# Attention scores for two light items at once, and the products with V of two items in front of them

## Chip, cores and metric

One core of one Trainium2 chip. The time is the device time of one execution in microseconds. The kernel before takes 2064.11 us, the median of three runs (2062.43 to 2066.58).

## What is computed

The input is x, 8 sequences of 1024 tokens with 256 features, in f32. Three residual blocks follow each other:

```
x = x + 0.5 * moe(layernorm(x))        # 8 experts of 128 hidden units, the best 2 per token
x = x + attention(layernorm(x))
x = x + 0.5 * moe(layernorm(x))
```

Attention has 8 heads of 64 and two branches whose outputs are added:

```
light: q, k, v = split(layernorm(x) @ wqkv); windows of 64 queries see 3 windows of 64 keys
       out = softmax(q k^T / 8) v @ wo_l                                    # all 1024 tokens
heavy: the 256 tokens with the highest scores x . rt_q are the queries,
       the 256 with the highest scores x . rt_kv are keys and values (rms-normed x)
       out = softmax(q k^T / 8) v @ wo_h, added back at the query tokens
```

## The kernel before

The program is written out by hand for the five engines (TensorE, ScalarE, VectorE, GpSimd, SyncE), with semaphores between them. The first block routes tokens to experts through memory (the first 371 us of the span), attention takes the time up to some 1610 us, and the last block computes all experts densely. The change touches attention alone.

Attention runs sequence after sequence, 0 to 7. A sequence has 40 items. An item is one tile of 128 queries and one pair of heads: 32 light items (8 tiles by 4 pairs) and then 8 heavy ones (2 tiles by 4 pairs). Each item sees 256 keys; for light ones a mask cuts the windows.

All engines walk through the same list of slots, `slots()`, one item per slot. In slot u:

- TensorE computes the scores of item u (`scores`, two heads, each with half of the array's rows: 64x128 tiles), the transposes of item u-3's probabilities (`turn`, full array) and the products with V of item u-4 (`values`, two heads, each with half of the array's columns: 128x64 tiles).
- VectorE adds the mask, copies the scores to `prob` and finds their maxima (`maxima(u)`), copies the turned probabilities of odd items from PSUM (`turned(u-3)`), and inverts the sums of item u-1.
- ScalarE computes the exponentials (`exps(u)`) and copies the turned probabilities of even items (`turned(u-3)`).
- GpSimd multiplies item u-1's probabilities with the inverse sums (`prob_norm`).

Between these stand jobs, listed per slot by `attn_jobs(u)`: projections to q, k and v of the same sequence and of the next (`qkv`), turned rows of the next sequence (`zt`), its routing scores (`srow`), the gather and the projections of the heavy branch (`ga`, `hp`), and the output product of a finished tile (`op`). TensorE does the first job of a slot after the scores, the second after the transposes, the others after the products with V. The jobs take PSUM banks 6 and 7 in turn, and `claim(job)` waits until the bank's job before the last has been copied out, mostly by ScalarE. A slot's jobs are the same in sequences 0 to 6 but for small shifts. Slots 2, 16, 18, 24, 30, 36 and 39 have none, slots 5, 9, 17, 27 and 33 only an output product or a heavy projection, slot 19 a gather, slots 20, 21, 23, 25 and 29 three or more. VectorE has, besides, the additions of the first block's results and the statistics for the next sequence (slots 1 to 19) and the ranking of tokens by pairwise comparison (`rank_piece`, slots 22 to 39 and 0 to 7). GpSimd has 16 gathers by indirect DMA in slots 35 to 39 and 0 to 10 and 16 scatters in slots 36 to 39, 0 to 3 and 9 to 16. Sequence 7 has no next one, so most of the jobs and of this other work are missing there.

The scores of item j, head h, go to `bank[g % NS]` with g = 2 * j + h and NS = 3, in columns 0 to 255. `scores(j)` waits for the reader of what the bank held before: score g - 3, that is the maxima (light) or the exponentials (heavy) of an item at most two before. `probT` has one buffer for even items and one for odd ones; `turn(j)` waits until item j-2's turned probabilities have been copied out of its bank, and the copy of item j waits for `values(j-2)`.

Of the kernel before, what the change touches and what calls it, by code (L numbers as in the profile page):

```python
# [31 lines left out]
LIGHT, SLOTS = 32, 40  # L32
# [6 lines left out]
def build(nc, x_in, gamma_h, wq_h, wkv_h, wo_h, ln_g, ln_b, wqkv, wo_l, rt_q, rt_kv,  # L39
# [4 lines left out]
    T = N // P  # L44
# [18 lines left out]
    MAXB, MAXI = max(BLOCKS), max(r1 - r0 for r0, r1 in BATCH) * N // BLK  # L63
    NH = 3
    NP = 4
    NS = 3
    assert FF == P and KEYS == NSEL and HC == 4 and TG == 4 and C == 2

    ctx = ExitStack()
    with ctx:  # L70
# [39 lines left out]
        mask = sb("mask", [P, 3, KEYS], BF16)  # L110
# [275 lines left out]
        def is_item(u):  # L386
            return 0 <= u < SLOTS * ROWS
# [91 lines left out]
        def tile_at(j):  # L479
            if not 0 <= j < 40 * ROWS:  # L480
                return None, None
            b, i = divmod(j, 40)
            return 10 * b + i // HP, i % HP

        def heavy_tile(n):
            return n % 10 >= T
# [241 lines left out]
        def pe_program():  # L728
# [232 lines left out]
            def scores(j):  # L961
                n, hp = tile_at(j)
                b, t = divmod(n, 10)
                if t < T:
                    if hp == 0 and t in (0, 3, 4):
                        pe.wait_ge(s_qkv, 25 * b + {0: qkv_with(0, 0), 3: qkv_with(1, 1), 4: qkv_with(0, 1)}[t])
                    if j == 0:
                        pe.wait_ge(s_halo, 2)
                        pe.wait_ge(s_by, STEPS)
                elif t == T and hp == 0:  # L970
                    pe.wait_ge(*left(("hp", b, 3)))
                for h in range(2):
                    g = 2 * j + h

                    if g >= NS:
                        if heavy_tile(tile_at((g - NS) // 2)[0]):
                            pe.wait_ge(s_soft, g - NS + 1)
                        else:
                            pe.wait_ge(s_nm, g - NS + 1)
                    hs = slice(h * DH, (h + 1) * DH)  # L980
                    if t < T:
                        ins = pe.matmul(bank[g % NS][:, 0:KEYS], qT[hs, hp, t * P:(t + 1) * P], kT[hs, hp, t * P:t * P + KEYS], start=True, stop=True)  # L982
                    else:
                        ins = pe.matmul(bank[g % NS][:, 0:KEYS], hq[hs, hp, (t - T) * P:(t - T + 1) * P], hk[hs, hp, :], start=True, stop=True)  # L984
                    ins.then_inc(s_sim)

            def turn(j):
# [73 lines left out]
                    job(*what)  # L1061
            for u in slots():
                todo = attn_jobs(u)
                if is_item(u):
                    scores(u)
                for what in todo[0:1]:
                    job(*what)
                if is_item(u - 3):
                    turn(u - 3)
                for what in todo[1:2]:  # L1070
                    job(*what)
                if is_item(u - 4):
                    values(u - 4)
                for what in todo[2:]:
                    job(*what)
                if u in EARLY.values():
                    ffn_hidden((u - SLOTS * ROWS) // 2)
            for k in range(GROUPS):
# [3 lines left out]
        def act_program():  # L1082
# [225 lines left out]
            def exps(j):  # L1308
                n, hp = tile_at(j)
                if j >= 4:  # L1310
                    act.wait_ge(s_rden, j - 3)
                light = n % 10 < T
                if not light:
                    act.wait_ge(s_tp, j - NP + 1)
                for h in range(2):
                    g = 2 * j + h
                    act.wait_ge(s_nm, g + 1)
                    src = prob[j % NP][:, h, :] if light else bank[g % NS][:, 0:KEYS]
                    act.activation(prob[j % NP][:, h, :], src, ACT.Exp, bias=nmax[:, j % 4, h:h + 1], scale=-1.0 if light else 1.0,  # L1319
                                   accum_out=den[:, j % 4, h:h + 1]).then_inc(s_soft)  # L1320

            def turned(j):

                if j % 2:
                    return
                act.wait_ge(s_tp, j + 1)
                if j >= 2:
                    act.wait_ge(s_pv, j - 1)
                act.activation(probT[j % 2][:, :, :], view(3 + j % 2, "p (a n) -> p a n", a=4), ACT.Copy).then_inc(s_pt[0])
# [49 lines left out]
            for u in slots():  # L1379
                todo = attn_jobs(u)  # L1380
                if is_item(u):
                    exps(u)
                for what in todo[0:1]:
                    evac(*what)
                if is_item(u - 3):
                    turned(u - 3)
                for what in todo[1:]:
                    evac(*what)
                if is_item(u - 4) and (u - 4) % HP == HP - 1:
                    values_left(tile_at(u - 4)[0])  # L1390
# [16 lines left out]
        def dve_program():  # L1407
# [360 lines left out]
            def maxima(j):  # L1768
                n, hp = tile_at(j)
                t = n % 10  # L1770
                if j >= 4:
                    dve.wait_ge(s_soft, 2 * (j - 3))
                if t < T and j >= NP:
                    dve.wait_ge(s_tp, j - NP + 1)
                which = 0 if t == 0 else 2 if t == T - 1 else 1
                for h in range(2):
                    g = 2 * j + h
                    dve.wait_ge(s_sim, g + 1)
                    if t < T:
                        ins = dve.tensor_tensor_reduce(prob[j % NP][:, h, :], bank[g % NS][:, 0:KEYS], mask[:, which, :], -1.0, 3e38, ALU.add, ALU.min, nmax[:, j % 4, h:h + 1])  # L1780
                    else:
                        ins = dve.tensor_reduce(nmax[:, j % 4, h:h + 1], bank[g % NS][:, 0:KEYS], AX_X, ALU.max, negate=True)
                    ins.then_inc(s_nm)

            def turned(j):

                if j % 2 == 0:
                    return
                dve.wait_ge(s_tp, j + 1)
                if j >= 2:  # L1790
                    dve.wait_ge(s_pv, j - 1)
                dve.tensor_copy(probT[j % 2][:, :, :], view(3 + j % 2, "p (a n) -> p a n", a=4)).then_inc(s_pt[1])  # L1792
# [350 lines left out]
```

## Time and profile before

| | |
|---|---|
| Median of three runs | 2064.11 us |
| The profiled execution | 2061.01 us, its span 2059.2 us |
| TensorE busy | 1875.1 us |
| VectorE busy | 1388.5 us |
| ScalarE busy | 1203.6 us |
| GpSimd busy | 1172.0 us |
| Mean granted clock of TensorE | 0.977 of 2.4 GHz |

The profile is one execution. A timeline row merges instructions of one line that follow each other without a gap; its first number is the start from the span's beginning. PEld is TensorE's weight load. A start of item 0's scores in a sequence marks the sequence's beginning: 371.00, 530.84, 690.43, 847.25, 1004.95, 1164.58, 1322.22 and 1479.02 us.

### The profile page before, as it was taken

How to read it: one execution, taken by the hardware profiler on the slowest of the kernel's cores; microseconds unless marked ns; L12 is line 12 of the kernel's file. 1: busy time of each engine (PE TensorE's matmuls, PEld its weight loads, DVE VectorE, ACT ScalarE, POOL GpSimd, SP SyncE). 2: the span in 40 equal slices, each digit the busy share in tenths (PEclk: the TensorE clock that was granted, in tenths of full speed). 3: DMA queues.
4: the chain of work that ended last, by engine and by line, in shares of the span. 5: the costliest groups of instructions: out<-in, count | busy, mean ns of one | idle time of the engine just before them, and what ended most of it. 6: DMA issues, size and time to landing. Idle time of an engine off the chain costs nothing.

```text
span 2059.2 us, 38092 instructions
## 1 busy us (share of the span) xinstructions
PE 1875.1 (91%) x11764; PEld 1398.7 (68%) x11764; DVE 1388.5 (67%) x4771; ACT 1203.6 (58%) x2974; POOL 1172.0 (57%) x1356
## 2 busy tenths in 40 slices
PE   3488899889989989989989989989999999999998
PEld 1166678656656666666666666666666788888887
DVE  5355457756855865875874875775754488888887
ACT  5487567565565565565566566566555555555554
POOL 3999852662772782782682683583453444444444
PEclk8599999999999999999999999999999999999999
DMA  6688887200310310310310220220121111111110
GB/s 200 248 267 289 275 267 251 67 27 1 100 40 1 98 42 1 95 45 1 93 47 1 81 55 5 77 57 8 37 63 82 38 42 42 42 42 42 36 38 21
DMA packets 103841, 168.15 MB, mean 82 GB/s; under 512 B 13249, under 2 KB 64857, under 8 KB 102745
## 3 DMA queue, kind: packets, MB, share of 16 engines
q1 hardware_dynamic: 80600, 112.91, 16.8%
q0 software_dynamic: 20736, 52.52, 8.1%
q8 instruction: 97, 1.59, 0.3%
q14 instruction: 104, 0.84, 0.1%
q10 hardware_dynamic: 2304, 0.28, 0.1%
HBM read 80.33 MB, written 85.34 MB: 80 GB/s over the span
## 4 chain that ended last, share of the span: by engine, by line
PE 51%; DVE 16%; POOL 10%; issue 10%; ACT 9%; DMA 4%; ACTq 0%; SPq 0%; DVEq 0%; POOLq 0%
PE bank L730 7%; PE bank L732 6%; PE bank L731 6%; PE bank L1022 4%; PE bank L1011 4%; PE bank L982 4%; PE bank L993 4%; PE bank L953 3%; PE bank L890 2%; ACT prob L1319 2%; PE bank L872 2%; POOL prob L2005 2%; DVE st L1412 2%; POOL spots_d L1952 2%; PE bank L984 2%
## 5 line engine op out<-in xcount | busy, mean ns | idle before, releaser
L2005 POOL TENSOR_TENSOR prob<-prob,rden 128x512 f32<-128x512 f32 x320 | 337.6, 1056 | 453.8 <-DVE rden L1798 450.2
L1319 ACT ACTIVATE prob<-prob,nmax 128x256 f32<-128x256 f32 x512 | 256.0, 502 | 391.3 <-DVE nmax L1780 383.5
L1780 DVE CUSTOM_DVE_ANT_0 prob<-bank,mask 128x256 f32<-128x256 f32 x512 | 195.3, 417 | 103.3 <-PE bank L982 97.3
L1666 DVE SCALAR_TENSOR_TENSOR xb<-bank,gate,xb 128x256 f32<-128x256 f32 x512 | 211.8, 476 | 55.6 <-PE bank L732 55.1
L1932 POOL TENSOR_TENSOR hl<-hf,hh 128x512 fp32r<-128x512 f32 x128 | 164.7, 1291 | 113.8 <-ACT hh L1122 109.1
L982 PE MATMUL bank<-kT,qT 64*128 64x256 f32 x1024 | 211.2, 431 | 14.3 <-DVE nmax L1780 13.6
L993 PE MATMUL bank<-ident,prob 128*128 128x128 f32 x1280 | 198.8, 278 | 16.1 <-POOL prob L2005 16.1
L993 PEld LDWEIGHTS bank<-ident,prob 128*128 128x128 f32 x1280 | 154.3, 142 | 73.7 <-POOL prob L2005 26.5
L1121 ACT ACTIVATE hf<-bank,b1s 128x512 f32<-128x512 f32 x128 | 88.2, 689 | 171.2 <-PE bank L732 167.7
L1792 DVE COPY probT<-bank 128x512 f32<-128x512 f32 x160 | 110.0, 688 | 113.7 <-PE bank L993 112.8
L1011 PE MATMUL bank<-probT,V 128*64 128x128 f32 x2048 | 169.7, 287 | 9.0 <-ACT oT_s L1335 7.1
L1992 POOL DMA_INDIRECT hs_d<-yr,place x128 | 130.0, 1016 | 43.4 <-issue 31.0
L1952 POOL DMA_INDIRECT spots_d<-xb,spot x128 | 126.3, 987 | 49.4 <-DVE spot L1513 28.4
L1011 PEld LDWEIGHTS bank<-probT,V 128*64 128x64 f32 x2048 | 108.2, 137 | 64.5 <-issue 61.3
L730 PE MATMUL bank<-w,hh 128*128 128x256 f32 x512 | 146.6, 286 | 3.7 <-POOL hl L1932 2.6
L982 PEld LDWEIGHTS bank<-kT,qT 64*128 64x128 f32 x1024 | 94.0, 186 | 77.7 <-issue 47.1
L732 PE MATMUL bank<-w,hh 128*128 128x256 f32 x512 | 144.7, 283 | 0.0
L731 PE MATMUL bank<-w,hl 128*128 128x256 f32 x512 | 144.5, 282 | 0.0
L1812 DVE TENSOR_TENSOR x<-bank,x 128x256 f32<-128x256 f32 x64 | 27.0, 422 | 147.0 <-PE bank L1022 147.0
L1578 DVE TENSOR_TENSOR yout<-bank,b_all 128x512 f32<-128x512 f32 x85 | 58.1, 690 | 100.5 <-PE bank L890 62.0
L1022 PE MATMUL bank<-wol,oT_s 128*128 128x256 f32 x512 | 125.8, 388 | 0.0
L730 PE MATMUL bank<-xt_hi,wqkv_hi 128*128 128x512 f32 x256 | 114.1, 446 | 0.0
(256 smaller groups left out, 5044.7 us busy)
## 6 DMA issues: line engine op xcount, KB each, us to landing
xin<-spots_d SPq DMA_DIRECT2D x85, 256.0 KB
made_d<-yout SPq DMA_DIRECT2D x85, 256.0 KB
x<-in_L_attn_x SPq DMA_DIRECT2D x8, 1024.0 KB
x_d<-x SPq DMA_DIRECT2D x8, 1024.0 KB, 4.5
xb<-x_d SPq DMA_DIRECT2D x16, 512.0 KB, 3.9
out<-xb SPq DMA_DIRECT2D x16, 512.0 KB, 3.0
xb<-in_L_attn_x SPq DMA_DIRECT2D x7, 1024.0 KB, 6.7
spots_d<-zeros SPq DMA_DIRECT2D x24, 256.0 KB
```

Of the source, the lines that this page charges most:

```text
L730: pe.matmul(o, w[0], x[0], start=start, stop=False)
L731: pe.matmul(o, w[1], x[0], start=False, stop=False)
L732: return pe.matmul(o, w[0], x[1], start=False, stop=stop)
L982: ins = pe.matmul(bank[g % NS][:, 0:KEYS], qT[hs, hp, t * P:(t + 1) * P], kT[hs, hp, t * P:t * P + KEYS], start=True, stop=True)
L993: ins = pe.transpose(bank[3 + j % 2][:, (2 * h + kk) * P:(2 * h + kk + 1) * P], prob[j % NP][:, h, kk * P:(kk + 1) * P], ident[:, :])
L1011: ins = pe.matmul(bank[5][h * DH:(h + 1) * DH, hp * P:(hp + 1) * P], V[:, t + kk, hs] if t < T else hv[:, kk, hs], probT[j % 2][:, 2 * h + ...
L1022: ins = pe.matmul(bank[tb][:, 0:D], oT_s[:, ch, :], w[:, ch, :], start=(ch == 0), stop=(ch == HC - 1))
L1319: act.activation(prob[j % NP][:, h, :], src, ACT.Exp, bias=nmax[:, j % 4, h:h + 1], scale=-1.0 if light else 1.0, accum_out=den[:, j % 4, ...
L1666: dve.scalar_tensor_tensor(out=x, in0=bank[ob][:, (t % 2) * D:(t % 2 + 1) * D], scalar=gate[:, k % 2, t, e:e + 1], in1=x, op0=ALU.mult, op ...
L1780: ins = dve.tensor_tensor_reduce(prob[j % NP][:, h, :], bank[g % NS][:, 0:KEYS], mask[:, which, :], -1.0, 3e38, ALU.add, ALU.min, nmax[:, ...
L1952: pool.indirect_dma_start(spots_d[batch_of_row(r)], bass.IndirectOffsetOnAxis(spot[:, r, c, t:t + 1], 0), xb[r % 4][:, t, :], None).then_i ...
L2005: pool.tensor_tensor(prob[j % NP][:, :, :], prob[j % NP][:, :, :], rden[:, j % 4, :].unsqueeze(2).broadcast_to([P, 2, KEYS]), ALU.mult).th ...
```

## The change

Light items 2i and 2i+1 form a set, and each heavy item is a set alone, 24 sets per sequence. A set uses two of the three banks, one per head; the even item of a light set writes columns 0 to 255, the odd one 256 to 511. TensorE computes the scores of both items in the even slot and none in the odd one. It waits, once per set and head, for the readers of what the banks held. VectorE's maxima wait until the set's last item has been computed for that head. The products with V of the two items u-5 and u-4 stand at the end of odd slots, after all jobs; in even slots there are none. All further jobs of a slot follow directly after the transposes. ScalarE copies the turned probabilities of even items one slot later, in slot u of item u-4, after the exponentials of slot u and ahead of all of its jobs. VectorE's copies of the odd items stay.

```diff
+        SETS = LIGHT // 2 + SLOTS - LIGHT
+        def set_of(j):
+            b, i = divmod(j, SLOTS)
+            return SETS * b + (i // 2 if i < LIGHT else i - LIGHT // 2)
+        def set_end(n):
+            b, i = divmod(n, SETS)
+            return SLOTS * b + (2 * i + 1 if i < LIGHT // 2 else i + LIGHT // 2)
+        def score_place(j, h):
+            n, side = ((0, 1), (2, 0), (1, 2))[set_of(j) % 3][h], 0 if heavy_tile(tile_at(j)[0]) else j % 2
+            return bank[n][:, side * KEYS:(side + 1) * KEYS]
...
                 for h in range(2):
-                    g = 2 * j + h
-                    if g >= NS:
-                        if heavy_tile(tile_at((g - NS) // 2)[0]):
-                            pe.wait_ge(s_soft, g - NS + 1)
-                        else:
-                            pe.wait_ge(s_nm, g - NS + 1)
+                    old = set_end(set_of(j) - 2 + h)
+                    if old >= 0 and (j == 0 or set_of(j - 1) != set_of(j)):
+                        pe.wait_ge(s_soft if heavy_tile(tile_at(old)[0]) else s_nm, 2 * old + (1 - h) + 1)
...
                 todo = attn_jobs(u)
-                if is_item(u):
-                    scores(u)
+                if is_item(u) and (u == 0 or set_of(u - 1) != set_of(u)):
+                    for j in range(u, set_end(set_of(u)) + 1):
+                        scores(j)
                 for what in todo[0:1]:
                     job(*what)
                 if is_item(u - 3):
                     turn(u - 3)
-                for what in todo[1:2]:
+                for what in todo[1:]:
                     job(*what)
-                if is_item(u - 4):
+                if u % 2 and is_item(u - 4):
+                    values(u - 5)
                     values(u - 4)
-                for what in todo[2:]:
-                    job(*what)
...
                 if is_item(u):
                     exps(u)
+                if is_item(u - 4):
+                    turned(u - 4)
                 for what in todo[0:1]:
                     evac(*what)
-                if is_item(u - 3):
-                    turned(u - 3)
...
                 for h in range(2):
                     g = 2 * j + h
-                    dve.wait_ge(s_sim, g + 1)
+                    dve.wait_ge(s_sim, 2 * set_end(set_of(j)) + h + 1)
```

The other lines put `score_place(j, h)` where `bank[g % NS][:, 0:KEYS]` stood.

## Rows read from the trace of the kernel before

**Rows 1.** The page's first part: busy time, share of the span, instructions of TensorE.

```profile
PE 1875.1 (91%) x11764; PEld 1398.7 (68%) x11764; DVE 1388.5 (67%) x4771; ACT 1203.6 (58%) x2974; POOL 1172.0 (57%) x1356
```

**Rows 2.** Stretches: length, busy time per engine (instructions), clock, DMA. Sequences 1, 3, 7.

```profile
530.84:690.43 159.59, 149.20 (x952) 103.25 (x951) 108.96 (x419) 94.61 (x271) 94.35 (x105) 0.99 0.16 46
847.25:1004.95 157.70, 147.23 (x952) 101.91 (x951) 108.59 (x419) 94.70 (x271) 94.45 (x105) 1.00 0.16 46
1479.02:1606.91 127.89, 124.26 (x850) 86.68 (x849) 69.34 (x282) 71.97 (x218) 60.68 (x61) 0.97 0.19 66
...
847.25:895.17 47.92, 46.37 (x294) 31.96 (x292) 42.43 (x163) 27.83 (x83) 39.91 (x46) 1.00 0.30 85
```

**Rows 3.** Timeline of TensorE, sequence 3, slots 14 and 15: start, length, what.

```profile
904.75 0.60 PE L993 MATMUL bank<-ident,prob 128*128 128x128 f32 x4
905.28 0.66 PE L1011 MATMUL bank<-probT,V 128*64 128x128 f32 x8
905.87 0.70 PE L982 MATMUL bank<-kT,qT 64*128 64x256 f32 x4
906.50 0.50 PE L730 MATMUL bank<-wqkv_hi,xt_hi 128*128 128x512 f32 x1
906.84 0.39 PE L731 MATMUL bank<-wqkv_hi,xt_lo 128*128 128x512 f32 x1
...
908.00 0.60 PE L993 MATMUL bank<-ident,prob 128*128 128x128 f32 x4
908.43 0.60 PE L900 MATMUL bank<-ident,z_row 128*128 128x128 f32 x4
```

**Rows 4.** Timeline, sequence 3, slots 22 and 23: TensorE, then VectorE, then ScalarE.

```profile
935.80 0.70 PE L982 MATMUL bank<-kT,qT 64*128 64x256 f32 x4
...
944.29 1.97 PE L953 MATMUL bank<-hin,wqh 128*128 128x256 f32 x8 [1.49 <-ACT kT L1276]
946.18 0.70 PE L982 MATMUL bank<-kT,qT 64*128 64x256 f32 x4
...
936.67 0.42 DVE L1780 CUSTOM_DVE_ANT_0 prob<-bank,mask 128x256 f32<-128x256 f32 x1 [0.27 <-PE bank L982]
...
938.57 0.69 DVE L1792 COPY probT<-bank 128x512 f32<-128x512 f32 x1 [1.12 <-PE bank L993]
...
942.06 0.41 DVE L1780 CUSTOM_DVE_ANT_0 prob<-bank,mask 128x256 f32<-128x256 f32 x1
...
942.57 0.51 ACT L1319 ACTIVATE prob<-prob,nmax 128x256 f32<-128x256 f32 x1 [3.80 <-DVE nmax L1780]
...
943.57 0.57 ACT L1276 ACTIVATE kT<-bank 128x512 f32<-128x512 f32 x1
944.04 0.58 ACT L1329 ACTIVATE probT<-bank 128x512 f32<-128x512 f32 x1
```

**Rows 5.** Timeline of TensorE, sequence 3, slots 12 and 13: transposes of items 9, 10.

```profile
894.00 0.66 PE L993 MATMUL bank<-ident,prob 128*128 128x128 f32 x4 [0.77 <-POOL prob L2005]
...
897.84 0.66 PE L993 MATMUL bank<-ident,prob 128*128 128x128 f32 x4 [1.38 <-POOL prob L2005]
```

**Rows 6.** Stretches around two long waits of TensorE; the third number from the end is the clock.

```profile
424.80:431.00 6.20, 3.90 (x15) 2.93 (x16) 0.86 (x6) 4.68 (x13) 3.12 (x4) 0.72 0.08 29
...
1543.00:1554.00 11.00, 7.63 (x31) 5.36 (x31) 4.89 (x24) 6.55 (x20) 3.71 (x6) 0.69 1.03 419
```

**Rows 7.** Timeline of TensorE behind the first of these waits.

```profile
427.13 0.76 PE L730 MATMUL bank<-wqkv_hi,xt_hi 128*128 128x512 f32 x1 [2.30 <-ACT xf_t L1265]
427.69 0.63 PE L731 MATMUL bank<-wqkv_hi,xt_lo 128*128 128x512 f32 x1
428.12 0.63 PE L732 MATMUL bank<-wqkv_lo,xt_hi 128*128 128x512 f32 x1
```

**Rows 8.** Timeline, sequence 3: maxima of item 18, then TensorE's scores of item 20.

```profile
918.28 0.42 DVE L1780 CUSTOM_DVE_ANT_0 prob<-bank,mask 128x256 f32<-128x256 f32 x1
...
921.01 0.83 PE L982 MATMUL bank<-kT,qT 64*128 64x256 f32 x4
```

More of the change, by code:

```diff
@@ L65, in build @@
     NP = 4
-    NS = 3
     assert FF == P and KEYS == NSEL and HC == 4 and TG == 4 and C == 2
@@ L972, in scores @@
                 for h in range(2):
-                    g = 2 * j + h
-                    if g >= NS:
-                        if heavy_tile(tile_at((g - NS) // 2)[0]):
-                            pe.wait_ge(s_soft, g - NS + 1)
-                        else:
-                            pe.wait_ge(s_nm, g - NS + 1)
+                    old = set_end(set_of(j) - 2 + h)
+                    if old >= 0 and (j == 0 or set_of(j - 1) != set_of(j)):
+                        pe.wait_ge(s_soft if heavy_tile(tile_at(old)[0]) else s_nm, 2 * old + (1 - h) + 1)
                     hs = slice(h * DH, (h + 1) * DH)
                     if t < T:
-                        ins = pe.matmul(bank[g % NS][:, 0:KEYS], qT[hs, hp, t * P:(t + 1) * P], kT[hs, hp, t * P:t * P + KEYS], start=True, stop=True)
+                        ins = pe.matmul(score_place(j, h), qT[hs, hp, t * P:(t + 1) * P], kT[hs, hp, t * P:t * P + KEYS], start=True, stop=True)
                     else:
-                        ins = pe.matmul(bank[g % NS][:, 0:KEYS], hq[hs, hp, (t - T) * P:(t - T + 1) * P], hk[hs, hp, :], start=True, stop=True)
+                        ins = pe.matmul(score_place(j, h), hq[hs, hp, (t - T) * P:(t - T + 1) * P], hk[hs, hp, :], start=True, stop=True)
                     ins.then_inc(s_sim)
@@ L1317, in exps @@
                     act.wait_ge(s_nm, g + 1)
-                    src = prob[j % NP][:, h, :] if light else bank[g % NS][:, 0:KEYS]
+                    src = prob[j % NP][:, h, :] if light else score_place(j, h)
                     act.activation(prob[j % NP][:, h, :], src, ACT.Exp, bias=nmax[:, j % 4, h:h + 1], scale=-1.0 if light else 1.0,
@@ L1777, in maxima @@
                     g = 2 * j + h
-                    dve.wait_ge(s_sim, g + 1)
+                    dve.wait_ge(s_sim, 2 * set_end(set_of(j)) + h + 1)
                     if t < T:
-                        ins = dve.tensor_tensor_reduce(prob[j % NP][:, h, :], bank[g % NS][:, 0:KEYS], mask[:, which, :], -1.0, 3e38, ALU.add, ALU.min, nmax[:, j % 4, h:h + 1])
+                        ins = dve.tensor_tensor_reduce(prob[j % NP][:, h, :], score_place(j, h), mask[:, which, :], -1.0, 3e38, ALU.add, ALU.min, nmax[:, j % 4, h:h + 1])
                     else:
-                        ins = dve.tensor_reduce(nmax[:, j % 4, h:h + 1], bank[g % NS][:, 0:KEYS], AX_X, ALU.max, negate=True)
+                        ins = dve.tensor_reduce(nmax[:, j % 4, h:h + 1], score_place(j, h), AX_X, ALU.max, negate=True)
                     ins.then_inc(s_nm)
```

## Prediction, written before the changed kernel ran

> **What bounds the kernel now.** I read the page first: TensorE is busy 91% of the span [rows 1], so the first question is which part of a slot on TensorE is work and which is not. The stretch table comes next [rows 2]: the whole of sequence 3 takes 157.70 us, of which TensorE is busy 147.23, VectorE 108.59, GpSimd 94.45. Its first twelve slots (47.92 us) look different: VectorE 42.43, GpSimd 39.91 and between GpSimd's DMA issues small gaps that nothing can fill. So slots 0 to 11 are held by three engines at once, slots 22 to 39 by TensorE. Sequence 7, which prepares no next sequence, needs 127.89 us with TensorE busy for 124.26. Last, the timeline of TensorE slot by slot [rows 3], and for single slots that of the other engines [rows 4, 5, 8].
>
> I number by the slot u of its sequence. S is the scores of an item, T its four transposes, V its product with V; "even" and "odd" are the slots of a pair.
>
> **What a change of the array's shape costs.** S uses 64x128 tiles, V 128x64, all else the full array. In [rows 3] T to V is 0.53 us, but T to another full-array group (908.00 to 908.43) 0.43: 0.10 lost on leaving. V takes 0.59 for eight instructions that run in pairs, four steps of 0.108, the step of T's transposes (0.43 for four): 0.15 lost (0.05 entering, 0.10 leaving). S takes 0.63 for two pairs of passes over 256 columns; eight such passes take 1.89 [rows 4], two 0.43: 0.20 lost. The projection's first pass takes 0.34 (906.50 to 906.84), the other five (908.00 - 906.84)/5 = 0.23: 0.10 lost. One round full array, V, S, full array costs 0.10 + 0.15 + 0.20 + 0.10 = 0.55 us, in each slot.
>
> The Trainium skill, TensorEngine Tiling (Array Packing), "Key Properties", says that a change of tiling mode drains the engine. The 0.10 on every leaving side agrees with it. By that rule alone this change is worth all the rounds that it takes out.
>
> **What the change removes.** Per pair of light items one of two rounds goes: 0.55. 128 pairs make 70 us. For heavy pairs only V moves; the round V to S of the even slot becomes T to S: some 0.15, 32 pairs, 5 us. A pair with a projection in each slot would fall from 6.49 to 5.94 us of TensorE time: S S 1.06, projection 1.50, T 0.43, projection 1.39, T 0.53, V V 1.02. This is the gross gain. The rest is what eats it.
>
> **What it adds.** (a) An even slot's maxima start when the second item's scores of that head are there: 0.87 us after S began now (935.80 to 936.67) [rows 4], 0.87 + 0.43 = 1.30 then. (b) T(u-3) of the even slot starts 0.43 later, and behind it VectorE's copy, its extras and the next maxima. (c) ScalarE copies T(u-4) only after exps(u). T(u-2) in the odd slot waits for that copy. Maxima to exps 0.51, two exps 1.00, copy 0.58 (942.06, 942.57, 943.57, 944.04) [rows 4], some 0.15 until TensorE starts: 1.30 + 2.24 = 3.55 us after S S began. With two projections T(u-2) comes at 4.39 and waits for nothing. With one it comes at 2.95 to 3.0, with none in the even slot and a gather in the odd one at 2.0. (d) V no longer stands between jobs. Where a job waits for its bank, V was done in that wait; now TensorE idles, and 1.02 us of V V follow. (e) Idle stretches merge and grow, and with them the clock. DMAs and GpSimd's commands are not moved; they follow the slots.
>
> **Slot by slot, for sequences 0 to 6** (plus is gain):
> Slots 36 to 11: VectorE and GpSimd set the pace [rows 2]; 0 (bounds -0.5 and +1.5; the second if all of S(0)'s gain went through).
> Slots 12, 13: T(9) at 894.00 and T(10) at 897.84 both wait for GpSimd [rows 5], whose chain is untouched. Between them stand now V(8), S(13) and a turn; then only the turn. The output product and V V come after T(10) and end before S(14) is wanted: 0 without the clock.
> Slots 14 to 19: two rounds 1.1, and a wait of V for ScalarE's copy of V's output goes, since V(4n) comes a slot later. But slot 18 has no job and 19 only a gather: maxima(18) at 918.28 [rows 8], T(16) 2.24 behind them, then T and V V, 1.55: S(20) at 922.1 minus what was won before, now 921.01. I take +0.3 up to S(22) without the clock.
> Slots 22, 23: maxima(23) stand behind the copy of T(19) and 3.5 us of rank work (938.57 to 942.06) [rows 4]. They shift by (b), 0.43. The heavy projection waits for the bank that ScalarE empties after exps(23), now at 944.29, 8.49 after S(22); then 8.9. It ends at 10.7, V V at 11.75, where S(24) began after 10.38: -1.4.
> Slots 24, 25: +0.55, less 0.6 by (c): 0. Slots 26 to 29: two rounds 1.1, less 0.4 for S(28), which waits for maxima behind two rank pieces: +0.7. Slots 30, 31: +0.95 with the present 0.5 wait of S(31) gone, less 0.6 by (c): +0.35. Slots 32 to 35: +0.3, given back in 36, 37, where S(37) comes 0.6 us before exps(36).
> Sum without the clock: 0.3 - 1.4 + 0 + 0.7 + 0.35 = 0 per sequence. Sequence 7 has little other work: 0.55 for each of seven pairs with full slots, 0.55 less some 0.28 by (c) for seven shorter ones, against 1.2 lost in the empty heavy slots by the wait of slot 37: +4.5.
>
> **The clock.** In the slot 22/23 pair TensorE has 1.06 + 1.50 + 0.43 + 1.39 + 0.43 + 0.43 = 5.25 us of work before the heavy projection and then stands for 8.9 - 5.3 = 3.6 us. In slots 12/13 it stands from 894.9 to 897.84, 2.9 us. Now the same places are waits of 1.49 and 1.38 [rows 4, 5], and sequence 3 has clock 1.00 [rows 2]. After a wait of 2.30 us [rows 7] the granted clock fell to the 1.2 GHz level: the projection's passes come 0.43 apart (427.69 to 428.12), not 0.23. The stretch around it has a mean of 0.72 [rows 6], so 0.28 x 2 x 6.2 = 3.5 us at half, 1.7 us of work lost; around the wait in sequence 7's slot 20 it is 0.69 over 11 us, 6.8 us at half, 3.4 lost. For slot 23 I take 2.2 (bounds 0 and 3.4): the work behind is dense and on the path. For slot 13 I take 0.8 (0 and 2): part of the loss falls into the wait for the claim of slot 14, the rest delays ScalarE's full queue there. That is 3.0 per sequence, 21 us for seven. Against it, sequences 0, 1 and 4 now lose 2 us each in slot 14 (159.6 against 157.7, clock 0.99 [rows 2]); that wait shrinks, as V V now fill it: +6.
>
> The Trainium skill, TensorE: Matmul & The Clock Gate, Part 1, says that a gap in the work sends the array back to the lower clock. The rows on the 2.30 us wait agree. It speaks against this change; by the tiling rule alone nothing of it would be seen.
>
> **Sum.** Loss 21 - 6 - 4.5 = 10.5 us. The profiled execution took 2061.01 us (span 2059.2), 3.1 under the median 2064.11 of the runs shown: 2071.5 there, 2074.5 as a median, forecast 2074.
>
> **Rivals.**
> 1. The clock holds, or falls in few sequences. For it: waits of 1.4 and 1.5 leave it at 1.00 [rows 2, 4, 5]. Against it: the 2.30 us wait. The shape rounds then stand alone: 0 x 7 + 4.5 + part of the 6: 8 us gained, 2056. Faster.
> 2. Both sides cancel: half of the falls, some sequences as now: within 4 us of 2064.
> 3. The rounds decide, since the waits of (b) to (d) overlap with waits that exist. With everything 1994; with the VectorE-bound and short slots taken out about half, 2030. Against it: VectorE 42.43 of 47.92 us in slots 0 to 11. For it: TensorE is busy 147.23 of 157.70 us. (The tiling rule of the skill alone gives this rival's first number.)
> 4. The fall lasts longer: each of 14 idle stretches costs 3.4, and ScalarE's queue in slots 14 to 21 never catches up: 14 x 3.4 - 10.5 = 37, less what lies in waits: 2090.
> 5. The change doesn't do what it says: V V or S S drain between items too. Nothing in [rows 3] shows that within one shape; it would take the 70 us away and leave the costs, over 2100.
>
> **Chances.** Forecast 0.55 (its own range 2067 to 2084), rival 1 0.19, rival 2 0.12, rival 3 0.06, rival 4 0.06, rival 5 0.02. What a measurement can tell from no change is 0.2%, 4.1 us. Slower: nearly all of the forecast, 4 and 5, 0.61; same: rival 2 and the forecast's lower edge, 0.14; faster: 1 and 3, 0.25. The range leaves out 3 and 5 and the end of 4: 2050 to 2090.
>
> **What would show it.** Right: TensorE idle for over 3 us before the heavy projection of slot 23 in seven sequences, and the granted clock under 1 behind it; S to maxima 1.30 in even slots; S S in 1.06 and V V in 1.02; slots 0 to 11 as long as now; sequence 7 shorter by some 4 us; no wait of V for the output copy in slot 16. Wrong: sequences under 156 us (then a drain was worth more, or the waits less), or a clock of 1.00 throughout, or V V over 1.2.

## Result and profile after

The changed kernel takes 2107.11 us (median of four runs, 2103.06 to 2110.6) against 2064.12: 1.0214 times as long, 95% interval 1.0196 to 1.0232. Forecast were 2074, range 2050 to 2090. The direction was right; the loss of 43 us is over four times the 10.5 forecast. The profiled executions differ by 49.0 us in span (2108.2 and 2059.2).

The page of after: its engine line, which answers to [rows 1], and the row of the transposes (busy us, mean ns | idle time ahead, what ended most of it).

```profile
PE 1848.6 (88%) x11764; PEld 1429.7 (68%) x11764; DVE 1399.4 (66%) x4771; ACT 1203.9 (57%) x2974; POOL 1173.3 (56%) x1356
...
L1008 PE MATMUL bank<-ident,prob 128*128 128x128 f32 x1280 | 204.3, 284 | 88.8 <-ACT probT L1346 60.1
```

TensorE is busy 26.5 us less, though a lower clock (mean 0.960, before 0.977) makes part of its work longer: the rounds that were taken out are gone. The same row on the page of before:

```profile
L993 PE MATMUL bank<-ident,prob 128*128 128x128 f32 x1280 | 198.8, 278 | 16.1 <-POOL prob L2005 16.1
```

The transposes wait 88.8 us instead of 16.1, and 60.1 of these end with ScalarE's copy of turned probabilities, which never released them before.

The stretches of after that answer to [rows 2]: sequences 1, 3, 7, then sequence 3 cut at the scores of items 12 and 22.

```profile
533.13:701.45 168.32, 147.05 (x952) 108.47 (x950) 110.75 (x419) 95.29 (x271) 94.53 (x105) 0.95 0.15 43
867.50:1036.28 168.78, 147.13 (x952) 108.50 (x950) 110.61 (x419) 95.35 (x271) 94.55 (x105) 0.95 0.15 43
1534.37:1656.48 122.11, 115.48 (x842) 85.52 (x840) 68.04 (x282) 69.16 (x215) 60.84 (x61) 1.00 0.20 69
...
867.50:915.92 48.42, 43.21 (x272) 32.06 (x271) 40.91 (x151) 23.75 (x71) 36.13 (x40) 0.93 0.30 83
915.92:965.51 49.59, 39.05 (x254) 29.66 (x252) 23.80 (x103) 33.80 (x90) 32.20 (x42) 0.90 0.11 30
965.51:1036.28 70.77, 64.88 (x430) 46.79 (x428) 45.90 (x166) 37.80 (x110) 26.21 (x26) 1.00 0.08 25
```

And of before, cut at the same items (the row of 47.92 us in [rows 2] ends one item later, at S of item 13):

```profile
847.25:890.47 43.22, 42.44 (x273) 29.49 (x271) 39.67 (x150) 23.63 (x71) 35.78 (x39) 1.00 0.33 94
890.47:935.80 45.33, 37.57 (x254) 26.09 (x252) 22.45 (x103) 33.75 (x91) 31.94 (x41) 1.00 0.12 33
935.80:1004.95 69.15, 67.23 (x429) 46.34 (x429) 46.48 (x169) 37.31 (x109) 26.73 (x26) 1.00 0.08 25
```

In sequence 3 slots 0 to 11 lose 5.2 us, slots 12 to 21 lose 4.3, slots 22 to 39 lose 1.6. As means over sequences 1 to 6 the losses are 4.5, 2.4 and 2.0 us: 8.8 per sequence, 53 in all. Sequence 0 loses 5.6, sequence 7 gains 5.8, what lies ahead of attention and behind it gains 3.9; together the 49.0. The largest part is where the prediction had put nothing, in slots 0 to 11.

**How slots 0 to 3 lose.** VectorE and GpSimd in slots 1 and 2 of sequence 3, before (start, length, what; L1750 is a rank operation, L1591 adds an expert's row, both read two inputs from SBUF; L1992 is GpSimd's scatter, L2005 its normalization):

```profile
851.67 0.35 DVE L1750 SCALAR_TENSOR_TENSOR sjunk<-srow,scol,not_later 128x128 uint8<-128x128 f32 x1
...
854.04 0.55 DVE L1591 SCALAR_TENSOR_TENSOR x<-y_row,share,x 128x256 f32<-128x256 f32 x1
...
851.88 1.01 POOL L1992 DMA_INDIRECT hs_d<-yr,place  x1 [0.30 <-issue]
852.92 1.05 POOL L2005 TENSOR_TENSOR prob<-prob,rden 128x512 f32<-128x512 f32 x1
```

And after (L1767, L1608, L2010, L2023 are the same four; L1798 at 880.35 is the maxima of item 2):

```profile
872.52 1.95 DVE L1767 SCALAR_TENSOR_TENSOR sjunk<-srow,scol,not_later 128x128 uint8<-128x128 f32 x1
...
876.35 1.79 DVE L1608 SCALAR_TENSOR_TENSOR x<-y_row,share,x 128x256 f32<-128x256 f32 x1
...
880.35 0.40 DVE L1798 CUSTOM_DVE_ANT_0 prob<-bank,mask 128x256 f32<-128x256 f32 x1
...
872.23 1.00 POOL L2010 DMA_INDIRECT hs_d<-yr,place  x1 [0.30 <-issue]
873.26 1.05 POOL L2023 TENSOR_TENSOR prob<-prob,rden 128x512 f32<-128x512 f32 x1
...
875.77 1.00 POOL L2010 DMA_INDIRECT hs_d<-yr,place  x1 [0.30 <-issue]
876.79 1.05 POOL L2023 TENSOR_TENSOR prob<-prob,rden 128x512 f32<-128x512 f32 x1
```

The rank operation began 0.21 us ahead of a scatter before and was done in 0.35. Now T(u-3) stands behind both items' scores, VectorE's copy of it comes later (4.08 us after S instead of 3.49), and the rank operation begins 0.29 us inside the scatter. It ends at 874.47, 0.16 behind the end of the normalization that follows the scatter (874.31). The same happens to the addition at 876.35: 1.79 instead of 0.55, ending 0.30 behind the next normalization. From the maxima of item 0 to those of item 2 it is 10.65 us instead of 7.77; the two operations are 1.60 and 1.24 us longer, together 2.84 of these 2.88. Item 2's exponentials follow the maxima, ScalarE's copy follows them by the changed order, and T(0), in slot 3, waits for the copy.

The Trainium skill, GPSIMD Engine Reference, "1. Specifications", says that GpSimd shares its SBUF interface with VectorE, and names two-input instructions of VectorE among those that contend. These rows agree, and add a size: up to 1.6 us for one operation. I had not weighed that rule, since the change adds no work to either engine; it only moves when they meet.

**What TensorE does then.** Its timeline in sequence 3 after, at the four places where it stands longest (the number in brackets is the idle time ahead): slots 3, 13, 19, 23.

```profile
882.57 0.63 PE L1008 MATMUL bank<-ident,prob 128*128 128x128 f32 x4 [3.42 <-ACT probT L1346]
...
884.39 2.66 PE L997 MATMUL bank<-kT,qT 64*128 64x256 f32 x8
...
923.19 0.66 PE L1008 MATMUL bank<-ident,prob 128*128 128x128 f32 x4 [2.75 <-POOL prob L2023]
...
945.88 1.09 PE L1008 MATMUL bank<-ident,prob 128*128 128x128 f32 x4 [3.64 <-ACT probT L1346]
...
974.41 1.97 PE L970 MATMUL bank<-hin,wqh 128*128 128x256 f32 x8 [3.46 <-ACT kT L1293]
```

The eight us behind each of these starts (third number from the end: mean granted clock):

```profile
882.57:890.57 8.00, 8.00 (x39) 5.98 (x40) 5.05 (x22) 4.23 (x12) 5.42 (x6) 0.58 0.22 69
923.19:931.19 8.00, 7.06 (x49) 5.56 (x50) 4.13 (x21) 5.27 (x15) 7.16 (x9) 1.00 0.23 49
945.88:953.88 8.00, 8.00 (x43) 5.99 (x44) 2.87 (x16) 5.50 (x15) 3.81 (x5) 0.61 0.01 3
974.41:982.41 8.00, 7.55 (x51) 5.84 (x52) 3.44 (x14) 5.03 (x14) 2.24 (x2) 1.00 0.01 2
```

The waits of slots 13 and 23 are nearly as forecast (2.9 and 3.6 us there), but the clock held behind both in this sequence. It fell behind those of slots 3 and 19, which the prediction doesn't have: the two pairs of scores at 884.39 take 2.66 us instead of 1.06. Over sequences 0 to 6 it fell behind slot 3 seven times, behind slot 19 five times of six waits over 2.7 us, behind slot 23 three times of seven, behind slot 13 twice of seven. Three more falls came in sequences 1, 3 and 5 behind a shorter wait, in slot 21 (in sequence 3 the clock fell at 958.94):

```profile
958.79 0.96 PE L917 MATMUL bank<-ident,z_row 128*128 128x128 f32 x4 [1.81 <-ACT srow L1303]
```

Attention as a whole runs 102.4 us at the 1.2 GHz level, before 23.9.

### The profile page after: what moved, and what is told of

It reads as the page before. It is cut to its first block, busy times and chain, and to the rows that moved or that the text cites. A ratio compares the mean times of both kernels' runs of the same rounds, so it can differ in the third digit from the quotient of the medians.

```text
span 2108.2 us, 38092 instructions
## 1 busy us (share of the span) xinstructions
PE 1848.6 (88%) x11764; PEld 1429.7 (68%) x11764; DVE 1399.4 (66%) x4771; ACT 1203.9 (57%) x2974; POOL 1173.3 (56%) x1356
## 4 chain that ended last, share of the span: by engine, by line
PE 45%; DVE 18%; issue 12%; POOL 10%; ACT 10%; DMA 3%; SPq 1%; DVEq 0%; ACTq 0%; POOLq 0%
PE bank L747 6%; PE bank L749 5%; PE bank L748 5%; PE bank L1026 5%; PE bank L997 5%; PE bank L1037 4%; PE bank L1008 3%; ACT prob L1336 3%; PE bank L970 2%; POOL prob L2023 2%; DVE x L1608 2%; DVE st L1429 2%; PE bank L907 2%; POOL spots_d L1970 2%; PE bank L999 1%
## 5 line engine op out<-in xcount | busy, mean ns | idle before, releaser
L2023 POOL TENSOR_TENSOR prob<-prob,rden 128x512 f32<-128x512 f32 x320 | 337.3, 1055 | 505.5 <-DVE rden L1816 500.0
L1008 PE MATMUL bank<-ident,prob 128*128 128x128 f32 x1280 | 204.3, 284 | 88.8 <-ACT probT L1346 60.1
L1798 DVE CUSTOM_DVE_ANT_0 prob<-bank,mask 128x256 f32<-128x256 f32 x512 | 194.9, 417 | 128.2 <-PE bank L997 127.7
L997 PE MATMUL bank<-kT,qT 64*128 64x256 f32 x1024 | 183.0, 422 | 11.9 <-DVE nmax L1798 9.9
L2010 POOL DMA_INDIRECT hs_d<-yr,place x128 | 130.0, 1016 | 43.6 <-issue 31.5
L1026 PE MATMUL bank<-probT,V 128*64 128x128 f32 x2048 | 147.8, 289 | 0.0
L997 PEld LDWEIGHTS bank<-kT,qT 64*128 64x128 f32 x1024 | 107.4, 195 | 58.2 <-issue 25.1
L1026 PEld LDWEIGHTS bank<-probT,V 128*64 128x64 f32 x2048 | 116.0, 143 | 34.2 <-issue 34.2
L1037 PEld LDWEIGHTS bank<-wol,oT_s 128*128 128x128 f32 x512 | 94.6, 194 | 35.2 <-issue 20.5
```

Source lines behind the costliest of these rows:

```text
L997: ins = pe.matmul(score_place(j, h), qT[hs, hp, t * P:(t + 1) * P], kT[hs, hp, t * P:t * P + KEYS], start=True, stop=True)
L1008: ins = pe.transpose(bank[3 + j % 2][:, (2 * h + kk) * P:(2 * h + kk + 1) * P], prob[j % NP][:, h, kk * P:(kk + 1) * P], ident[:, :])
L1026: ins = pe.matmul(bank[5][h * DH:(h + 1) * DH, hp * P:(hp + 1) * P], V[:, t + kk, hs] if t < T else hv[:, kk, hs], probT[j % 2][:, 2 * h + ...
L1037: ins = pe.matmul(bank[tb][:, 0:D], oT_s[:, ch, :], w[:, ch, :], start=(ch == 0), stop=(ch == HC - 1))
L1798: ins = dve.tensor_tensor_reduce(prob[j % NP][:, h, :], score_place(j, h), mask[:, which, :], -1.0, 3e38, ALU.add, ALU.min, nmax[:, j % 4, ...
L2023: pool.tensor_tensor(prob[j % NP][:, :, :], prob[j % NP][:, :, :], rden[:, j % 4, :].unsqueeze(2).broadcast_to([P, 2, KEYS]), ALU.mult).th ...
```

## Experiments

A ratio is to the kernel before, timed on the same chip. "Slots 0-11" and the like are means over sequences 1 to 6 of the profiled execution; before has 42.9 us in slots 0-11, 46.0 in 12-21, 69.1 in 22-39, and after 47.5, 48.4, 71.0. "M0 to M2" is from the maxima of item 0 to those of item 2 in the same way: before 7.99, after 10.66.

### The first half alone: scores in pairs (ss_only)

V and ScalarE's copy go back to their places:

```diff
-                for what in todo[1:]:
+                for what in todo[1:2]:
                     job(*what)
-                if u % 2 and is_item(u - 4):
-                    values(u - 5)
+                if is_item(u - 4):
                     values(u - 4)
+                for what in todo[2:]:
+                    job(*what)
...
-                if is_item(u - 4):
-                    turned(u - 4)
                 for what in todo[0:1]:
                     evac(*what)
+                if is_item(u - 3):
+                    turned(u - 3)
```

> The first half of the change alone: the scores of two light items together, with the banks and waits of the change; the products with V in every slot and ScalarE's copy of the even items where they were before. Of a pair's rounds only the odd slot's V to S goes, 0.20 us, 128 pairs, 25 us of TensorE work. Theory (the loss of the change comes from the second half: T(u-2) waits for a copy that stands behind exps(u), V V stand exposed behind waiting jobs, and the idle stretches that result drop the clock): sequence 7 gains about 3 us, sequences 0 to 6 lose little, total 2050 to 2066. Rival (the loss comes from the 0.43 us by which maxima and T(u-3) of even slots are later, and from the collisions of VectorE with GpSimd that this shifts): sequences 0 to 6 are 3 us longer each, total 2080 to 2090.

Measured: 2077.43 us, 1.0100 (1.0083 to 1.0117). Slots 0-11 take 46.2 us (+3.3), 12-21 46.0, 22-39 68.5 (-0.5). The time lies outside both ranges; the rival comes nearer, with 2.7 us per sequence where it had 3. Pairing the scores alone makes the kernel slower, and in slots 0-5 in the main: M0 to M2 is 10.72 us in sequence 3, as long as in after (10.65). So the late copy of ScalarE isn't needed for that loss.

One sequence of this kernel escapes it. In sequence 2 the M0 to M2 time is 7.99 us and slots 0-11 take 43.5, where the five others have 10.71 to 10.74 and 46.4 to 47.6. The rank operation of slot 1 and the scatter beside it, sequence 2 and then sequence 3:

```profile
696.48 0.35 DVE L1767 SCALAR_TENSOR_TENSOR sjunk<-srow,scol,not_later 128x128 uint8<-128x128 f32 x1
...
696.37 1.06 POOL L2010 DMA_INDIRECT hs_d<-yr,place  x1 [0.30 <-issue]
```

```profile
854.21 1.98 DVE L1767 SCALAR_TENSOR_TENSOR sjunk<-srow,scol,not_later 128x128 uint8<-128x128 f32 x1
...
853.96 1.00 POOL L2010 DMA_INDIRECT hs_d<-yr,place  x1 [0.31 <-issue]
```

In sequence 2 the operation begins 0.11 us into the scatter and isn't held, in sequence 3 it begins 0.25 us into it and takes 1.98. The order of the instructions is the same, and GpSimd's normalization behind the scatter comes no earlier in sequence 2 (5.83 us after S(0), 5.65 in sequence 3). The held operations are thus what makes M0 to M2 long.

### The other half alone: V in pairs, the late copy (vv_only)

The scores are single again, with `bank[g % NS]` and its wait as before; V and ScalarE's copy stay as changed.

> The second half alone: scores in every slot with three banks as before; V of two items at the end of odd slots after all jobs, and ScalarE's copy of even items a slot later behind the exponentials. Theory (second half carries the loss): T(u-2) waits, slot 23 idles over 3 us, the clock falls; 2085 to 2100. Rival (first half carries it): 2060 to 2070.

Measured: 2070.25 us, 1.0052 (1.0035 to 1.0069). Slots 0-11 43.9 (+1.0), 12-21 46.7 (+0.6), 22-39 69.7 (+0.6, of it +1.8 in slots 22/23 and -1.4 in 24 to 35). The time is at the edge of the rival's range, far from the theory's 2085. Both halves lose, and less than the whole: 1.00% and 0.52% against 2.14%.

### ScalarE's copy ahead of the exponentials (copy_first)

```diff
+                if is_item(u - 4):
+                    turned(u - 4)
                 if is_item(u):
                     exps(u)
-                if is_item(u - 4):
-                    turned(u - 4)
```

> The changed kernel with one edit: ScalarE copies the turned even item of slot u ahead of the exponentials of slot u, not behind them. What it copies has been ready since the slot before. T(u-2) then no longer waits for maxima(u) and exps(u). Theory (this wait is the largest single part: 3.4 us idle in slot 3, 3.6 in slot 19, both with a fall of the clock behind them): 12 to 25 us below the changed kernel, 2082 to 2095. Rival (VectorE is as late in these slots anyway, the wait moves to the next scores, which need the maxima): within 4 us of 2107.

Measured: 2100.2 us, 1.0211 (1.0194 to 1.0229), by the ratio as after, as the rival had it. The wait of slot 3 goes (slots 2/3 take 6.3 us instead of 8.9), and slots 4/5 take 11.6 instead of 7.9: VectorE's chain of maxima is as late as in after. TensorE from V V of slot 3 to the scores of slot 4, sequence 3 of this kernel:

```profile
876.07 0.66 PE L1026 MATMUL bank<-probT,hv 128*64 128x128 f32 x8 [1.59 <-DVE probT L1810]
876.66 0.70 PE L997 MATMUL bank<-kT,qT 64*128 64x256 f32 x2
879.28 2.07 PE L997 MATMUL bank<-kT,qT 64*128 64x256 f32 x6 [1.93 <-DVE nmax L1798]
```

The copy was only the last link. VectorE's copy and maxima now stand there as the releasers, and the scores run at half clock again (2.07 us for six passes).

### Work for TensorE in the waits (filler)

```diff
+            def busy(u, n):
+                k = set_of(u)
+                pe.wait_ge(s_nm, 2 * set_end(k - 1) + 2)
+                for _ in range(n):
+                    pe.matmul(bank[(2, 1, 0)[k % 3]][:, 0:KEYS], ident[:, :], wol_s[:, 0, :], start=True, stop=True)
+            FILL = {3: 7, 13: 6, 19: 7}
...
+                if SLOTS <= u < LAST and u % SLOTS in FILL:
+                    busy(u, FILL[u % SLOTS])
...
+                    if SLOTS <= u < LAST and u % SLOTS == 23 and what[0] == "hp":
+                        busy(u, 7)
```

> The changed kernel, and in sequences 1 to 6 TensorE multiplies into an unused bank while it would wait: 7 products of 0.43 us ahead of the transposes of slots 3 and 19, 6 ahead of those of slot 13, 7 ahead of the heavy projection of slot 23. Outputs are not changed. Every wait stays; only the idle time is filled. Theory (the lower clock behind the idle stretches carries about half of the loss: 106 us at the lower level in attention against 27 before): the granted clock stays at 1.00 in sequences 1 to 6 and the time falls by 15 to 35 us, to 2072 to 2092. Rival (the lower clock falls into other waits and costs little, the waits themselves are the loss): 2100 to 2110.

Measured: 2086.52 us, 1.0139 (1.0119 to 1.0160), clock 0.976, 27.3 us of attention at the lower level, none of it in sequences 1 to 6. Against after's ratio of 1.0214, taken on another chip, that is 0.75% or some 15 us (by the two intervals 7 to 23); the two profiled executions differ by 26 us in sequences 1 to 6. That is what the falls cost, those of slot 21 among them, which went too. The prediction's clock terms came to 15 net (21 lost, 6 given back): the order of size stands, its places don't.

The rest of the loss, about half of it or more, stands at full clock. Slots 0-11 take 45.8 us in this kernel (+2.9 on before), 12-21 take 46.3 (+0.2), 22-39 take 70.5 (+1.4). So 1.7 of the 4.5 us in slots 0-11 and nearly all of the loss in 12-21 go with the clock.

### V in pairs in front of the waiting job (vv_inside)

```diff
-                for what in todo[1:]:
+                for what in todo[1:2]:
                     job(*what)
                 if u % 2 and is_item(u - 4):
                     values(u - 5)
                     values(u - 4)
+                for what in todo[2:]:
+                    job(*what)
```

> As after, but in odd slots the two products with V stand behind the first of the jobs that follow the transposes, and the rest of the jobs behind them, so that they fill the wait of that job for its bank. Theory 'exposed V V' (point (d) of the prediction): in slots 22/23 the idle time before the heavy projection takes V V in, 1.0 us back there, as much in each other pair whose last job waits (12/13, 20/21): 1.5 to 3 us per sequence, 10 to 20 us in all, 2088 to 2098, and the granted clock rises since the longest idle stretches are cut by 1 us. Rival 'the wait is set elsewhere': what waits is the chain maxima, exps, bank, which V V do not touch, and the job they now stand in front of is late by 1 us: within 4 us of after's 2107, slots 12/13 and 22/23 no shorter than now (11.5, 12.4 us).

Measured: 2088.18 us, 1.0121 (1.0098 to 1.0144): 19 us under after. Point (d) of the prediction, V exposed behind a waiting job, is thus worth 0.9%. The prediction charged it in slots 18/19 and 22/23 alone. Slots 20/21 fall from 15.6 to 13.7 us (1.0 us under the 14.7 of filler) and 22/23 from 12.4 to 11.3. Slots 12/13 don't (11.5, 11.7): what waits there is T(10) itself, behind GpSimd, and V V still follow it. TensorE in slot 23 of sequence 3 in this kernel:

```profile
957.50 1.09 PE L1026 MATMUL bank<-probT,V 128*64 128x128 f32 x16
961.06 3.54 PE L970 MATMUL bank<-hin,wqh 128*128 128x256 f32 x8 [2.46 <-ACT kT L1294]
```

V V now lie in the wait, which is 2.46 us instead of 3.46. But here the clock fell behind it (3.54 us for the projection, 1.97 in after) and took the gain back in this sequence. A shorter wait doesn't guarantee the clock.

### Without the scatters (before_ns, after_ns)

```diff
                 for b, i in due(u, scatter_slot, 2 * T):
-                    scatter(b, i // T, i % T)
+                    if b in (0, ROWS - 1):
+                        scatter(b, i // T, i % T)
```

(The waits on the scatters' counts go down with them, in both kernels.)

> Before, without the 96 scatters of rows that GpSimd issues for sequences 1 to 6 (each 1.0 us of GpSimd; the selected rows of sequence 0 are read in their place, so part of the computation is left out). Theory 'GpSimd holds VectorE's operations': slots 0 to 11 of sequences 1 to 5 shrink from 42.9 us by 2 to 6 us. It is the base for after_ns, its slots are to be compared with those.

> After, without the same 96 scatters. Theory 'collision': what the change lost in slots 0 to 11 (4.5 us per sequence) came from VectorE's operations being held longer behind scatter and normalization of GpSimd; without scatters after_ns stands there within 1.5 us of before_ns, and the ratio after_ns to before_ns is under 1.012. Rival 'waits alone': slots 0 to 5 are longer because T(u-2) waits for ScalarE's copy and the maxima stand behind VectorE's later copy; the difference stays at 3.5 us or more per sequence, ratio 1.018 or more.

Measured: before_ns 2065.56 us, 1.0015 (1.0003 to 1.0026); after_ns 2093.25 us, 1.0152 (1.0128 to 1.0175). after_ns stands 1.37% over before_ns, between the two thresholds (1.2% and 1.8%). Slots 0-11 take 42.2 and 43.6 us: of the change's 4.5 us there 1.5 are left, in this point as the collision theory had it. M0 to M2 is 7.25 and 7.40. VectorE and GpSimd in after_ns, the same two operations as above:

```profile
864.62 1.12 DVE L1767 SCALAR_TENSOR_TENSOR sjunk<-srow,scol,not_later 128x128 uint8<-128x128 f32 x1
...
867.62 0.48 DVE L1608 SCALAR_TENSOR_TENSOR x<-y_row,share,x 128x256 f32<-128x256 f32 x1
...
864.53 1.06 POOL L2023 TENSOR_TENSOR prob<-prob,rden 128x512 f32<-128x512 f32 x1 [1.82 <-DVE rden L1816]
...
866.75 1.05 POOL L2023 TENSOR_TENSOR prob<-prob,rden 128x512 f32<-128x512 f32 x1
```

Without a scatter ahead of it a normalization holds an operation for its own length at most (1.12 us, ending 0.15 behind it), and the addition is free. Three things limit this result. Slots 12-21 don't profit (47.9 and 48.8 us, where before has 46.0 and after 48.4): in before_ns slots 12/13 gain 2.1 us and slots 14/15 lose 4.3, with a fall of the clock there in every sequence. The sum of the stretching, VectorE's operations of attention with two inputs in SBUF against the shortest tenth of their kind, is no smaller without scatters (96 us in before, 109 in before_ns, 107 in after, 108 in after_ns): other operations are caught. What counted was which, on the way to the next maxima. And taking scatters out also makes GpSimd's first five normalizations of a sequence 1.0 to 2.5 us earlier, which this pair of kernels can't separate from the collision; sequence 2 of ss_only, above, does.

### The change in sequence 7 alone (last_only)

```diff
         def set_of(j):
+            if j < LAST:
+                return j
...
+                if 0 <= u - 4 < LAST:
+                    values(u - 4)
...
-                if u % 2 and is_item(u - 4):
+                if u % 2 and LAST <= u - 4 and is_item(u - 4):
                     values(u - 5)
                     values(u - 4)
```

> The change in sequence 7 alone; sequences 0 to 6 keep the order of before. Theory 'rounds pay where TensorE alone sets the pace': sequence 7 is 5.8 us shorter as in after (127.9 to 122.1), all else as before: 0.28% faster than before, ratio 0.9972. Rival 'sequence 7 only gains by work that the slower sequence 6 had left done': the gain is under 2 us, ratio over 0.999.

Measured: 2056.52 us, 0.9972 (0.9959 to 0.9985), as the first theory had it: 0.28% faster. Where TensorE alone sets the pace the change is a gain. A full pair of sequence 7 in after:

```profile
1583.53 0.60 PE L1008 MATMUL bank<-ident,prob 128*128 128x128 f32 x4
1584.06 1.09 PE L1026 MATMUL bank<-probT,V 128*64 128x128 f32 x16
1585.08 1.13 PE L997 MATMUL bank<-kT,qT 64*128 64x256 f32 x8
1586.15 0.66 PE L1008 MATMUL bank<-ident,prob 128*128 128x128 f32 x4
```

V V 1.02 us, S S 1.07: with [rows 3] as the singles, the round is worth the 0.55 us that the prediction took. Pairs 4 to 14 of sequence 7 are 0.53 to 0.56 us shorter each.

### Sequence 7, and the late slots of the others (ss_late, vv_late)

```diff
+        def paired(j):
+            i = j % SLOTS
+            return i < LIGHT and (j >= LAST or True and i >= 24)
...
+        def values_paired(j):
+            return j >= LAST or False and 20 <= j % SLOTS < 36
...
+        def copied_late(j):
+            return j >= LAST or False and 20 <= j % SLOTS < 38
```

This is ss_late. In vv_late the first condition has False and the two others True. ScalarE's copy is thus late in vv_late for item 36 too, and falls into slot 0 of the next sequence.

> Sequence 7 as after; in sequences 0 to 6 only the scores of slots 24 to 31 are paired (four pairs, no scatter, no command of GpSimd there), V and ScalarE's copies as before. Theory 'pairs pay where TensorE sets the pace': in ss_only slots 24 to 31 were 1.3 us shorter than before; 7 x 1.3 + 5.8 for sequence 7 = 14.7 us, ratio 0.993. Rival 'given back': slots 32 to 39 or the next sequence's first slots, whose claim and rank work do not move, wait as much longer; only sequence 7's part is left, ratio 0.997.

> Sequence 7 as after; in sequences 0 to 6 only the products with V of items 20 to 35 go in pairs at the end of their odd slots (ScalarE's copy a slot later there), scores single as before. Theory 'pairs pay where TensorE sets the pace': in vv_only slots 24 to 35 were 1.4 us shorter than before; its loss in slots 22, 23 (V V of items 18, 19 behind the heavy projection) does not arise; 7 x 1.4 + 5.8 = 15.6 us, ratio 0.9925. Rival 'given back': the late copy holds T(u-2) at the start of slots 36, 37, or the next sequence waits as much longer: ratio 0.997.

Measured: ss_late 2047.9 us, 0.9941 (0.9928 to 0.9954); vv_late 2052.21 us, 0.9955 (0.9942 to 0.9969). Slots 22-35 are 1.2 and 1.4 us shorter than before. In ss_late slots 0-11 and 36-39 stay as they were (42.8, 12.3); in vv_late 1.0 and 0.2 us are given back there (43.9, 12.5), which puts its time between theory and rival. That isn't the waiting that the rival had in mind. V(36) now waits for the late copy in slot 0 of the next sequence, here sequence 3:

```profile
845.25 0.66 PE L1038 MATMUL bank<-probT,hv 128*64 128x128 f32 x8 [0.75 <-ACT probT L1362]
```

Everything behind it comes later against GpSimd's scatters, and M0 to M2 is 9.70 us, 1.4 of it in held operations, though nothing of slots 1 to 11 was changed. The stretch from the scores of item 24 to those of item 32, sequence 3, before and in ss_late:

```profile
946.18:979.26 33.08, 32.99 (x199) 22.14 (x198) 21.32 (x86) 17.71 (x52) 9.73 (x9) 1.00 0.00 1
```

```profile
937.65:969.52 31.87, 31.87 (x199) 22.42 (x198) 20.95 (x83) 16.83 (x51) 9.40 (x9) 1.00 0.00 1
```

TensorE is busy for the whole of either stretch, and GpSimd for less than a third. Here TensorE's busy time falls by 1.1 us and the stretch by 1.2. ss_late beats both kernels, before by 0.6%.

## Why the prediction missed

**Slots 36 to 11, "VectorE and GpSimd set the pace; 0 (bounds -0.5 and +1.5)".** This is the step that failed. Measured: -4.5 in slots 0-11 and -0.25 in 36-39, per sequence. The first clause was right, and it should have ruled out the second. That two engines set the pace means that a shift of one against the other counts; the prediction asked what becomes of TensorE's gain and took VectorE's and GpSimd's chains as fixed. Point (b), 0.43 us later for VectorE's copy, stood in the text and was charged in slots 22/23 and, as 0.4, at S(28), but not here. In place of 0 the runs show this: the paired scores shift VectorE against GpSimd's scatters, two held operations make M0 to M2 2.9 us longer, and the clock falls behind the wait of slot 3 that comes of it (1.7 us, by filler). ss_only shows that the paired scores alone make three quarters of the loss (3.3 of 4.5), the no-scatter pair that two thirds of it hang on the scatters, and sequence 2 of ss_only that without the held operations M0 to M2 is as before.

**Point (c), T(u-2) waits for ScalarE's copy at 3.55 us.** The chain was right, but sized with the maxima of the even slot at 1.30 us after S. In slots 2/3 they come at 4.3, so T(0) comes at 6.5. Only slots with maxima on time obey the 3.55.

**Slots 12, 13: 0 without the clock.** Measured -1.2 as a mean, but -0.35 in each of the four sequences of 1 to 6 where the clock held: nearly right. T(10)'s wait is 2.75 us, where 2.9 was forecast. In sequences 2 and 6 the clock fell, and the pair took 2.7 us more, of which 1.0 came back in slots 14/15. **Slots 14 to 21: +0.3 without the clock.** Measured -1.1, and +0.1 in filler, where the clock held. The near hit is luck: pairs 14 and 16 gain 2.3 and 0.2, pair 18 takes 8.0 us instead of 5.2. The chain was right (T(16) 2.24 us behind maxima(18) in sequence 3, as worked out), but these maxima came 3.68 us after S(18) and not 2.34. The routing products in front of them were held again; in sequence 3 before and after, in the same order:

```profile
913.30 1.02 DVE L1720 CUSTOM_DVE_ANT_0 scj<-y_row,rts 128x256 f32<-128x256 f32 x1
...
916.99 0.79 DVE L1720 CUSTOM_DVE_ANT_0 scj<-y_row,rts 128x256 f32<-128x256 f32 x1
```

```profile
938.03 1.65 DVE L1737 CUSTOM_DVE_ANT_0 scj<-y_row,rts 128x256 f32<-128x256 f32 x1
...
941.76 1.37 DVE L1737 CUSTOM_DVE_ANT_0 scj<-y_row,rts 128x256 f32<-128x256 f32 x1
```

The falls behind that wait and in slot 21 did the rest: with filler pair 18 takes 7.5 us, and pair 20 14.7 instead of 15.6.

**Slots 22, 23: -1.4.** The heavy projection waits 3.46 us in every sequence, and the pair takes 1.44 us more where the clock holds: right. **Slots 24 to 39.** Forecast 0, +0.7, +0.35 and 0 (sum +1.05), measured -0.3, -0.1, +0.35 and +0.05 (sum 0). Slots 28/29 lose 0.7, with copy_first too, so it isn't the copy: both maxima come 1.0 us later, of which (b) explains 0.43. With V V inside (vv_inside) slots 28/29 take 10.2 us as before, but 30/31 then take 0.5 more; where the other half comes from stays open.

**The clock.** Forecast 15 us net, found some 15 by the ratios and 26 by the profiled executions. By places it was wrong: two waits per sequence, each with a fall, against four long waits, falls behind 17 of 27 of them, and three more in slot 21. A fall behind slot 23 costs 1.6 us (2.2 forecast), and it comes in three sequences of seven. That the total is near is luck. The Trainium skill, TensorE: Matmul & The Clock Gate, Part 1, by which a gap sends the array back to the lower clock, was weighed as if each gap over 2.3 us did. The runs agree that the clock falls behind gaps, but not behind each: waits of 2.75 us in slot 13 kept the clock in five sequences of seven, those of 3.46 in four. The traces of before had shown it already: waits of 1.80 us in slot 14 dropped the clock in two sequences (1 and 4) and kept it in three (2, 3 and 6).

**Sequence 7: +4.5.** Measured 5.8. The time lies beyond **rival 4**, and no fall in slots 13 to 23 costs its 3.4 us. **Rival 3**, that the rounds decide, is what holds there and in the late slots of ss_late; **rival 5** is out, since V V and S S run without a drain between items.

## What to carry to other kernels

Taking work off the busiest engine by changing its order paid here only in the stretches where that engine alone is late; cut a change by stretch before taking or dropping it, as ss_late did with one that lost 2.1% as a whole. Where two other engines set the pace, list for each of their instructions that is moved what the other runs at that moment: a shift of 0.4 us cost 2.9 here, and one of 0.14 us decided over 2.7 in ss_only. A wait behind a copy must be followed back to the latest maxima in front of it, slot by slot, not from a typical slot.

## What the runs showed of the hardware

- A VectorE operation with two inputs in SBUF that starts while GpSimd issues a scatter, with a normalization right behind, can be held until that normalization has ended: 1.95 us instead of 0.35, 1.79 instead of 0.55, ending 0.16 and 0.30 us behind it. It isn't always so. In the attention of after there are 28 such operations: none of the nine that began in the first 0.17 us of the scatter was held, and 18 of the 19 that began from 0.27 us on were, by 1.06 to 1.62 us. In before five that began 0.24 to 0.31 us into it weren't. Beside a scatter with no GpSimd operation right behind it none was (10 in before, 9 in after). Beside a normalization alone the operation of 0.35 us took 1.12.
- TensorE's clock did not fall behind every wait of one length: behind 3.42 to 3.45 us in slot 3 six times of six, behind 3.46 us in slot 23 three of seven, behind 2.75 us in slot 13 two of seven, behind 1.81 us in slot 21 three of three, and in before behind 1.80 us in slot 14 two of five. What tells them apart stays open.
- Products of 256 columns in an unused bank, in the waits, kept the clock at 2.4 GHz in sequences 1 to 6 and gave back 0.75%.
